# A sandwich layer on one core: when x of batches 2 and 3 is normalised, transposed and split

## The reference

```python
def _layernorm(x, axis=-1, eps=1e-05):
    m = jnp.mean(x, axis=axis, keepdims=True)
    v = jnp.var(x, axis=axis, keepdims=True)
    return (x - m) / jnp.sqrt(v + eps)
...
        q = (hidden_states @ Wq).reshape(b, s, HEADS, HEAD_DIM)      # 16 heads of 64
        k = (hidden_states @ Wk).reshape(b, s, HEADS, HEAD_DIM)
        v = (hidden_states @ Wv).reshape(b, s, HEADS, HEAD_DIM)
        # q and k are rotated by position (rotary embedding)
        logits = jnp.einsum('bhqd,bhkd->bhqk', q, k)
        logits = jnp.where(causal, logits, MASK_VAL)
        logits = logits / jnp.sqrt(jnp.float32(HEAD_DIM))
        attn = jax.nn.softmax(logits, axis=-1)
        out = jnp.einsum('bhqk,bhkd->bhqd', attn, v)
        return out @ Wo
...
        scores = H * jax.nn.softmax(router_logits, axis=-1)          # 8 experts of rank 16
        low = jnp.einsum('bsd,hrd->bshr', x, A)
        out = jnp.einsum('bshr,hor,bsh->bso', low, B, scores)
...
    x = x + _layernorm(attention(_layernorm(x)))
    x = x + _layernorm(experts(_layernorm(x)))
```

## Time and profile before

| | |
|---|---|
| median of three runs | 1184.49 us |
| the profiled execution | 1184.45 us |
| its span in the profile | 1182.7 us |
| TensorE busy (matmul) | 1089.5 us, 92% |
| DVE, ACT, POOL busy | 756.7, 628.3, 438.3 us |

### The profile page before, as it was taken

The page is one execution under the profiler, slowest core; times in us unless marked ns, Lnnn a source line. Parts: engine busy times, 40 slices in busy tenths (PEclk is TensorE's granted clock), DMA queues, the critical chain, the costliest instruction groups (busy, mean ns, idle before and its releaser), DMA issues.

```text
span 1182.7 us, 20255 instructions
## 1 busy us (share of the span) xinstructions
PE 1089.5 (92%) x5616; PEld 905.7 (77%) x5616; DVE 756.7 (64%) x2075; ACT 628.3 (53%) x1435; POOL 438.3 (37%) x412
## 2 busy tenths in 40 slices
PE   2899999999999776899999999999976999999984
PEld 2688888888888664688888888888865888888873
DVE  7656666666666675666666666666664666666663
ACT  4445555555555545555555555555564454544542
POOL 3053543535435232153543535435253223323311
PEclk9999999999999988999999999999989999999995
DMA  5111101111012113011101101010424132333210
GB/s 213 54 36 33 63 13 62 44 31 62 14 61 82 43 59 98 5 50 28 62 24 51 49 27 62 27 48 14 134 63 140 57 104 95 101 106 106 84 40 36
DMA packets 37499, 73.44 MB, mean 62 GB/s; under 512 B 3152, under 2 KB 19536, under 8 KB 37456
## 3 DMA queue, kind: packets, MB, share of 16 engines
q1 hardware_dynamic: 37456, 72.92, 19.0%
HBM read 56.14 MB, written 16.78 MB: 62 GB/s over the span
## 4 chain that ended last, share of the span: by engine, by line
PE 78%; DVE 8%; ACT 6%; issue 6%; DMA 1%; POOL 1%; POOLq 0%; DVEq 0%; SPq 0%; ACTq 0%
PE bank L1076 40%; PE bank L1034 30%; PE bank L1103 5%; ACT prob L591 1%; PE bank L1055 1%; PE bank L1195 1%; DVE prob L833 1%; DVE big_lo L822 1%; ACT pT_hi L602 1%; DVE q_hl L865 1%; DVE stats L776 1%; DVE stats L777 1%; DVE rr L797 1%; ACT xn L561 1%; DMA w_raw<-in_wqkv 1%
## 5 line engine op out<-in xcount | busy, mean ns | idle before, releaser
L1076 PE MATMUL bank<-big_hi,w_hi 128*128 128x512 f32 x768 | 335.9, 437 | 16.1 <-DVE big_lo L822 13.4
L474 POOL TENSOR_SCALAR prob<-prob,rinv 128x128 f32<-128x128 f32 (+3 forms) x256 | 156.6, 612 | 508.6 <-DVE rinv L843 508.6
L591 ACT ACTIVATE prob<-prob,nmax 128x128 f32<-128x128 f32 (+3 forms) x256 | 143.6, 561 | 353.4 <-DVE nmax L833 352.1
L1076 PE MATMUL bank<-big_hi,w_lo 128*128 128x512 f32 x768 | 306.4, 399 | 0.0
L1076 PE MATMUL bank<-big_lo,w_hi 128*128 128x512 f32 x768 | 304.4, 396 | 0.0
L1076 PEld LDWEIGHTS bank<-big_hi,w_hi 128*128 128x128 f32 x768 | 147.5, 192 | 33.7 <-issue 17.5
L1076 PEld LDWEIGHTS bank<-big_hi,w_lo 128*128 128x128 f32 x768 | 146.2, 190 | 34.4
L851 DVE TENSOR_TENSOR pT_lo<-bank,pT_hi 128x128 fp32r<-128x128 f32 (+3 forms) x256 | 123.9, 484 | 57.4 <-ACT pT_hi L602 54.1
L1076 PEld LDWEIGHTS bank<-big_lo,w_hi 128*128 128x128 f32 x768 | 148.4, 193 | 12.0
L843 DVE RECIPROCAL rinv<-rsum 128x1 f32<-128x1 f32 x256 | 40.8, 160 | 159.2 <-ACT prob L591 159.1
L833 DVE CUSTOM_DVE_ANT_0 prob<-bank,mask 128x128 f32<-128x128 f32 (+3 forms) x256 | 124.3, 486 | 22.3 <-PE bank L1034 18.4
(11 more groups left out here) (106 smaller groups left out, 1921.4 us busy)
## 6 DMA issues: line engine op xcount, KB each, us to landing
w_raw<-in_wqkv SPq DMA_DIRECT2D x48, 512.0 KB, 3.6
attention_out<-o_sum SPq DMA_DIRECT2D x64, 128.0 KB, 2.3
xin<-attention_out SPq DMA_DIRECT2D x16, 512.0 KB, 4.8
xres<-in_x SPq DMA_DIRECT2D x16, 512.0 KB, 3.5
out<-res SPq DMA_DIRECT2D x16, 512.0 KB, 2.6
xin<-in_x SPq DMA_DIRECT2D x14, 512.0 KB, 3.7
w_raw<-in_wo SPq DMA_DIRECT2D x6, 512.0 KB, 4.3
prob<-in_x SPq DMA_DIRECT2D x2, 512.0 KB, 7.7
```

Of the source, the lines that this page charges most:

```text
L474: pool.tensor_scalar(p, p, rinv[:, q % 4:q % 4 + 1], 1.0, ALU.mult, ALU.mult).then_inc(prob_done, 1)
L591: act.activation(prob[:, q % 4, 0:n], prob[:, q % 4, 0:n], ACT.Exp, scale=-1.0, bias=nmax[:, q % 4:q % 4 + 1], accum_out=rsum[:, q % 4:q % ...
L1076: done = pe.matmul(grp_ps[(b + k) % 2][:, :], w, xt, start=at == 0, stop=at == GROUP_MM - 1)
```

## The change

Eight tiles, 8 to 15, are the x of batches 2 and 3. In the kernel after, tile 8 is handled in slot 2, tile 9 in slot 3, and so on to tile 15 in slot 9 (`ahead_tile`, `AHEAD`). In such a slot SP loads the tile first; DVE takes its statistics at the end of step 2; ACT and DVE scale and ACT normalises it at the end of step 4; TensorE, ACT and DVE transpose and split its two chunks at the end of steps 5 and 6 (`hold_chunk`), through the same bank `tr_ps`, but into two spare buffers in SBUF (`hold_hi`, `hold_lo`); SP then stores these to two DRAM tensors, 512 KB each (`hold_x`). What stood in slots 14, 15 and 16 for these tiles is gone. When unit 14 is through, SP loads the parts of batch 2 back in four DMAs of 1 MB (`load_xT`), and when unit 15 is through those of batch 3. TensorE waits for these loads in slots 16 and 17. The pairs 1 to 4 of the first half get a loop of their own.

```diff
+EARLY = TILES // 2
+AHEAD = EARLY // 2
+PART = KC // 2
...
+        xT_hold = [nc.dram_tensor(f"xT_hold_{n}", (P, KC, 2 * SEQ), F32, kind="Internal").ap() for n in ("hi", "lo")]
...
+        hold_hi = xin[:, 1, :].rearrange("p (c t) -> p c t", c=KC)
+        hold_lo = xn[:, 1, :].rearrange("p (c t) -> p c t", c=KC)
...
         def x_turns(u, s):
-            now = {0: 1, UPH - 1: 2, UPH: 3}.get(u)
-            nxt = {UPH - 2: 2, UPH - 1: 3}.get(u)
...
+            if not isinstance(u, int) or u != 0:
+                return [], []
+            return [4 + s // 2 + 2] if s in (1, 3) else [], [s]
+        def ahead_tile(u):
+            return u + EARLY - 2
...
+                if half == 0:
+                    with eng.Fori(1, AHEAD + 1) as pair:
+                        slot(pair, 0, half, True)
+                        slot(pair, 1, half, True)
+                with eng.Fori(1 if half else AHEAD + 1, PAIRS - 1) as pair:
...
+            def hold_x(n, fill):
+                sp.wait_ge(tr_lo, fill + 3)
+                for kept, staged in zip(xT_hold, (hold_hi, hold_lo)):
+                    sp.dma_start(kept[:, :, bass.ds((n - EARLY) * P, P)], staged).then_inc(held, 16)
+            def load_xT(b):
+                sp.wait_ge(held, 32 * EARLY + 32)
+                sp.wait_ge(grp_done, 3 * (UPH - 2 + b) + 3)
+                for i in range(2):
+                    for kept, xT in zip(xT_hold, (xT_hi, xT_lo)):
+                        sp.dma_start(xT[:, b, PART * i:PART * i + PART, :].bitcast(F32), kept[:, PART * i:PART * i + PART, SEQ * b:SEQ * b + SEQ]
+                                     ).then_inc(xT_in[2 * b + i], 16)
...
+                if isinstance(u, int) and u in (UPH - 1, UPH):
+                    load_xT(u - UPH + 1)
+                if ahead:
+                    load_x(ahead_tile(u))
                 if more:
                     load_w(0, n, nxt)
...
                 store_o(u - 2, stored[0], b, stored[1], 1)
+                if ahead:
+                    hold_x(ahead_tile(u), v_fill(u, half, ahead))
...
# ACT
+            def hold_chunk(u, c, fill):
+                act.wait_ge(tr_done, fill + c + 2)
+                if c == 0:
+                    act.wait_ge(held, 32 * (u - 1))
+                act.activation(hold_hi[:, PART * c:PART * c + PART, :].bitcast(F32R),
+                               tr_ps[:, :].rearrange("p (c t) -> p c t", c=PART), ACT.Copy).then_inc(tr_hi, 1)
...
+                    if ahead and s == 4:
+                        ln_start(ahead_tile(u))
                     pt_high(u, s)
...
+                    if ahead and s == 4:
+                        x_normal(ahead_tile(u))
+                    if ahead and s in (5, 6):
+                        hold_chunk(u, s - 5, fill)
...
# DVE
+            def hold_chunk(u, c, fill):
+                dve.wait_ge(tr_hi, fill + c + 2)
+                if c == 0:
+                    dve.wait_ge(held, 32 * (u - 1))
+                at = (slice(None), slice(PART * c, PART * c + PART), slice(None))
+                dve.tensor_tensor(hold_lo[at].bitcast(F32R), tr_ps[:, :].rearrange("p (c t) -> p c t", c=PART),
+                                  hold_hi[at], ALU.subtract).then_inc(tr_lo, 1)
...
+                    if ahead and s == 2:
+                        x_variance(ahead_tile(u))
+                    if ahead and s == 4:
+                        ln_scale(ahead_tile(u))
+                    if ahead and s in (5, 6):
+                        hold_chunk(u, s - 5, fill)
...
# TensorE
+            def hold_chunk(u, c, fill):
+                pe.wait_ge(normed, ahead_tile(u) + 1)
+                pe.wait_ge(tr_hi, fill + c + 1)
+                pe.wait_ge(tr_lo, fill + c + 1)
+                for k in range(PART):
+                    col = P * (PART * c + k)
+                    last = pe.transpose(tr_ps[:, P * k:P * k + P], xn[:, 0, col:col + P], ident[:, :])
+                last.then_inc(tr_done, 1)
...
+                    if isinstance(u, int) and u in (UPH, UPH + 1) and k == 0 and part == 0 and c % PART == 0:
+                        pe.wait_ge(xT_in[2 * b + c // PART], 32)
```

More of the change, by code:

```diff
@@ L168, in sandwich_kernel @@
         tr_lo = sem("tr_lo")
+        held = sem("held")
+        xT_in = [sem(f"xT_in{i}") for i in range(4)]
         w_hi_done = [sem(f"w_hi_done{m}") for m in range(3)]
@@ L368, in load_xres @@
                 sp.dma_start(xres[:, i, :], x[bass.ds(t * P, P), :]).then_inc(xres_in[i], 16)
+            sp.sem_inc(held, 32)
             load_x(0)
@@ L380, in _, with slot @@
                 load_x(n)
-            def slot(pair, b, half):
+            def slot(pair, b, half, ahead=False):
                 u = 2 * pair + b + UPH * half
@@ L404, in slot @@
                     load_oT(3, 1)
[L406 to L409, removed]
+                if isinstance(u, int) and u == 0:
+                    load_x(6)
                 store_o(u - 2, stored[0], b, stored[1], 0)
-                for t in later.get(u, ()) if isinstance(u, int) else ():
-                    load_x(t)
+                if isinstance(u, int) and u == 0:
+                    load_x(7)
                 if more:
@@ L635, in o_lower, with slot @@
                 act.activation(o_low[:, :], o_ps[DH:2 * DH, :], ACT.Copy).then_inc(olow_done, 1)
-            def slot(pair, b, half):
+            def slot(pair, b, half, ahead=False):
                 u = 2 * pair + b + UPH * half
                 n = pair + PAIRS * half
-                fill = v_fill(u, half)
+                fill = v_fill(u, half, ahead)
                 for s in range(STEPS):
-                    batch, tiles, chunks = x_turns(u, s)
+                    tiles, chunks = x_turns(u, s)
                     exponent(u, s)
@@ L915, in slot @@
                     for c in chunks:
-                        x_chunk(batch, c)
+                        x_chunk(1, c)
+                    if ahead and s == 2:
[4 more added lines that the diff above has]
+                        hold_chunk(u, s - 5, fill)
                     if isinstance(u, int) and u == UNITS and s % 2 == 0:
@@ L1164, in slot @@
                     if s == 0:
-                        attend(u - 2, b, 0, v_fill(u - 1, half) + 1)
+                        attend(u - 2, b, 0, fill)
                     if s == 4:
                         attend(u - 2, b, 1, None)
-                    batch, _, chunks = x_turns(u, s)
+                    _, chunks = x_turns(u, s)
                     for c in chunks:
-                        x_chunk(batch, c)
+                        x_chunk(1, c)
+                    if ahead and s in (5, 6):
+                        hold_chunk(u, s - 5, fill)
                     if isinstance(u, int) and STEPS * u + s in range(STEPS * UNITS + 2, STEPS * UNITS + KC + 2):
```

51 lines of the change are left out of this document (18 added, 33 removed).

## The result

The kernel after took 1192.89 us, the median of four runs (1191.81 to 1195.76), against 1184.57 us for the kernel before in the same session (1184.37 to 1185.08). The ratio is 1.0073 with a 95% interval of 1.0055 to 1.0091: slower by 8.3 us. The profiled execution took 1193.17 us, its span is 1191.3 us, 8.6 us more than before.

A forecast was written before the change was run, and what follows sets the result against it. The prediction took the ACT-DVE chain (maximum, exponential, reciprocal, next maximum) as the bound, not TensorE. It added 4 x 5.9 + 4 x 8.1 + 1 = 57.0 us, removed 48.4, and forecast 1193 us from 1184.45, range 1181 to 1200.

The forecast's parts named there:

- The chain decides: Ordinary slots: ACT and DVE answering each other set 49.20 us a pair; TensorE's own period is 48.76 us.
- Rival 2: Slots 2 to 9: chain has slack, tile work fits DVE's idle time; 4 us added, 1140 us; chance 0.13.
- What is removed: Slots 14 to 17: tile work leaves slots 14 to 16, saving 48.4 us if x is loaded in time.
- What is added, even slots: Even slots of 2 to 9: tile work and two chunks cost 5.9 us each.
- statistics, scaling, normalising: Steps 2 and 4 of slots 2 to 9: 3.47 us a slot, ACT's share included.
- first chunk: End of step 5, slots 2 to 9: DVE's subtraction pushes the next maximum by 0.61 us.
- second chunk: End of step 6, slots 2 to 9: ACT's uncovered copy and DVE's subtraction delay the maximum by 1.8 us.
- What is added, odd slots: Odd slots of 2 to 9: POOL blocks DVE's low part of q in step 4, 2.2 us more, 8.1 each.
- Low clock: Slots 2 to 9: after waiting for the tile TensorE runs slower; 0.25 us in four slots, 1 us in all.
- Transfers: Tile stores and loads in slots 2 to 9, batch reloads: 0 counted, high end 3 us a slot.
- Rival 3: Slots 2 to 9: late stores or low clock cost 3 us more in 6 slots or so; 1208 us; chance 0.12.
- rival 1: Odd slots: DVE starts ahead of POOL, port free, 5.9 us each; 1184.3 us, no change; chance 0.2.

The follow-up runs named there:

- g1: Kernel before plus one unused DVE statistics operation at the end of step 2 in slots 18 to 29: 1191.99 us, ratio 1.0058.
- g2: Kernel before plus one unused DVE statistics operation in step 1, between maximum and low sum of the output, slots 18 to 29: 1184.97 us, ratio 1.0.
- f2: Kernel after with tile work moved into engine waits, loads earlier, and TensorE's step 0 product not waiting for the second chunk: 1146.09 us, ratio 0.9674.
- e4: Kernel after without tile work in slots 2 to 9; x of batches 0 and 1 stored and loaded back instead: 1134.98 us, ratio 0.9581.
- e2: Kernel after with ACT's and DVE's part of the second chunk at the end of step 7 instead of 6: 1186.21 us, ratio 1.0011.
- e5: Kernel after with DVE's scaling in step 4 between maximum and reciprocal, ACT's logarithm and exponential in step 3: 1173.22 us, ratio 0.9906.
- e1: Kernel after with ACT's logarithm and exponential of the tile behind the high probabilities in step 4, slots 2 to 9: 1190.92 us, ratio 1.0043.

## Why the prediction was right, and where it was off

**The chain decides.** "The chain maximum, exponential, reciprocal, next maximum runs round without rest, and whatever is put between its links on DVE lengthens every slot by its full length." Shown by g1: 0.6 us ahead of a maximum cost 0.58 us a slot. As it stands the sentence is too wide, since g2's operation is also between two links, the maximum and the reciprocal, and costs nothing: what lengthens a slot is work between ACT's answer and the next maximum, and all that the change adds on DVE stands there. f2 shows both sides for the whole tile. The reading that TensorE does not bind, though it is never idle, holds too. These are its transposed v of units 1, 6, 9 and 11 in the kernel before:

```profile
85.67 0.60 PE L1055 MATMUL bank<-ident,raw 128*128 128x128 f32 x4
...
207.54 0.60 PE L1055 MATMUL bank<-ident,raw 128*128 128x128 f32 x4
...
281.31 0.60 PE L1055 MATMUL bank<-ident,raw 128*128 128x128 f32 x4
...
330.49 0.60 PE L1055 MATMUL bank<-ident,raw 128*128 128x128 f32 x4
```

The first two are five units apart, 24.37 us each; the last two are a pair, 49.18 us, the pace of the chain. So TensorE goes for a while at a shorter pace of its own and then takes the chain's; its busy time, 196.65 of 196.78 us in slots 2 to 9, does not tell the two apart.

Rival 2, slack in the chain, is out for the places that the change uses. It would have been right for places between the maximum and the reciprocal; the prediction's "DVE's idle time is the time in which it waits for ACT's answer" was used only to say that the time is lost, not that it can be filled.

**What is removed.** Predicted 48.4 us, measured 48.75 in the kernel after, with e4 as the proof that nothing else hangs on it.

**What is added, even slots.** Predicted 5.9 us each, measured 6.2 to 6.3, and 7.0 in slot 4. Slot 6 has the three terms one by one, between the marks that the prediction used. First the kernel before, from the low part of the probabilities of step 5 on, then the kernel after:

```profile
199.55 0.66 DVE L851 TENSOR_TENSOR pT_lo<-bank,pT_hi 128x512 fp32r<-128x512 f32 x1
...
201.62 0.29 DVE L851 TENSOR_TENSOR pT_lo<-bank,pT_hi 128x128 fp32r<-128x128 f32 x1
```
```profile
215.83 0.69 DVE L923 TENSOR_TENSOR v_hl<-bank,v_hl 128x512 fp32r<-128x512 f32 x1 [0.32 <-ACT v_hl L660]
...
227.95 0.56 DVE L898 TENSOR_TENSOR pT_lo<-bank,pT_hi 128x384 fp32r<-128x384 f32 x1 [0.97 <-ACT pT_hi L635]
...
231.48 0.66 DVE L898 TENSOR_TENSOR pT_lo<-bank,pT_hi 128x512 fp32r<-128x512 f32 x1
...
235.34 0.29 DVE L898 TENSOR_TENSOR pT_lo<-bank,pT_hi 128x128 fp32r<-128x128 f32 x1
```

| term | before | after | cost | predicted |
|---|---|---|---|---|
| statistics, scaling, normalising | 8.34 | 12.12 | 3.78 | 3.47 |
| first chunk | 2.93 | 3.53 | 0.60 | 0.61 |
| second chunk | 2.07 | 3.86 | 1.79 | 1.8 |

The whole 0.3 is in the first term. Of it 0.2 is a pause that the prediction had not counted: the maximum of step 3, which now stands right behind a tile's statistics, starts 0.19 us late, put down to issue (the row at 219.04 above is that of slot 6; seven such waits, 1.3 us in all). The cause of the other 0.1 us stays open. For the second chunk e2 confirms the price: it takes 1.2 of it away and leaves the subtraction.

**What is added, odd slots.** Predicted 8.1 us, measured 8.4. The 2.2 us for POOL's block came out as 2.17 on the operation (2.85 against 0.68) and 2.05 by e5. That DVE would come second again, by 0.03 us, was taken over from slot 15, and it did, four times of four. The rule of the Trainium skill that was weighed there (SBUF — State Buffer, Who interferes with whom: the second to start waits for the end of the first) is borne out by these traces in either order: q takes 2.85 us behind POOL in the kernel after, and in e1 0.87 us ahead of POOL, whose own operation then takes 2.77 us instead of 2.34.

**Low clock.** Predicted 1 us in four slots, measured 0.7 in one. TensorE waited for the tile by 3.2 to 6.9 us in each of eight slots, and the granted clock of the stretch is 0.93, but only in slot 4 was TensorE late for the chain: 30.17 us against some 29.45 in the other even slots. There its granted clock stood at 0.50, the lower of its two levels, for 6 us from the end of its wait (162.1 to 168 us), twice as long as the case that the prediction started from; in slot 6, after a wait as long (4.0 us), for 3 us. Slot 4 is the one place where ACT waits for TensorE (timeline of ACT):

```profile
167.07 0.60 ACT L635 ACTIVATE pT_hi<-bank 128x512 fp32r<-128x512 f32 x1 [0.67 <-PE bank L1166]
```

**Transfers.** Predicted 0, and right: the two stores of a tile land in 3.6 and 5.4 us. The next load is issued 1.6 us behind the first store and lands 5.7 us later, 7.3 us in all (7.8 where it takes 6.2), just under the lower of the two estimates, 7.9 us. DVE waits for no load, and slots 14 to 17 take 98.02 us with the reload on the way. Rival 3 is out.

**The sum.** Predicted +57.0 - 48.4 = +8.6, measured in the span +59.2 - 48.75 = +10.4, less 2.45 us in the opening, which the change does not touch, and plus 0.6 us behind slot 18: +8.6 in the profiled execution, +8.3 by the medians. The closeness of the total is partly luck: the additions were 2.2 us too low and the opening gave 2.45 us back, most of it by a clock that was full in slot 1 of this trace. Three sums of the prediction are slightly off and decide nothing: 3 us in six slots are 18 us, not 15 (rival 3 would be at 1211); a pair in rival 1 is 49.2 + 11.8 = 61.0 us, not 60.8; and 6 us for the low clock give an upper bound of 1198, not 1199.

**Rival 1 was priced wrongly.** It said that with the port free the kernel would stand at 1184.3, since the four odd slots would lose 2.2 us each. e1 is just this case, DVE first, and it stands at 1190.9. The step that failed is that only the low part of q can be hit: the operation behind it, tiny as it is, took the block over. With the right price the rival would have been another form of slower, and the chance for no change should have been smaller.

## What to carry to other kernels

Where two engines answer each other in turn, the engine's idle time is a particular place in its program, between its question and the other's answer: work that needs no answer goes there and is free up to the length of that wait, and the same work a few instructions further down is paid in full. A feeding engine that is 100% busy at the full clock does not show that it binds; look whether anyone in the chain ever waits for it. Moving an operation ahead of the one that blocks it frees little if another of the same kind comes next and takes the block (e1); with the operations behind it moved out of the way as well, it paid (e5).

## What the runs showed of the hardware

A scalar_tensor_tensor of DVE on one value per partition took 0.22 us alone and 2.18 us when it started 0.60 us behind POOL's low part of the weights (e1). So an operation this small can be blocked for 1.96 us, nearly as long as the 64x512 one (2.17 us), and the trace counts the block as busy time. Three operations of such size behind it (0.15, 0.16 and 0.16 us) ran after POOL had ended and were not hit. And the busy time of DVE in slots 2 to 9 differs by 8.1 us between the kernel after and e5 for the same instructions, so that a stretch's busy sum is not a measure of its work.
